# A state-space block with its FFN: one pass of TensorE per unit, the scores in three PSUM banks, y beside the states

## The reference, cut to what matters

```python
h = layernorm(x) * (1 + ca) + sa                      # x: (4, 512, 256)
proj = h @ W_in.T                                     # x, B, C, z, A_log
xBC = conv over 4 taps along l, per channel, + conv_b
a = -softplus(A_log)                                  # 32 heads
Lm = exp(segsum(a))                                   # l x s, lower triangle
M = einsum('blhn,bshn,bhls->bhls', Cm, Bm, Lm)        # 64 states per head
y = einsum('bhls,bshp->blhp', M, x) + D * x           # 8 channels per head
x = x + ga * ((y * silu(z + z_bias)) @ W_out.T)
h = layernorm(x) * (1 + cb) + sb
x = x + gb * (fwht(silu(h @ W1.T) * (h @ W3.T)) @ W2.T)
```

## Time and profile before

| what | value |
|---|---|
| median of 3 runs | 541.29 us (541.1 to 541.99) |
| the profiled execution's own time | 541.1 us |
| its span | 538.9 us |
| TensorE's granted clock, mean | 0.996 |
| busy: PE, DVE, ACT, POOL | 528.2, 455.3, 372.5, 241.0 us |

### The profile page before, as it was taken

One profiled execution on the slowest core, in us unless ns is written; L12 is line 12 of the kernel. 1 busy time (PEld: TensorE's weight loads), 2 busy tenths in 40 slices (PEclk: granted clock), 3 DMA queues, 4 the chain that ended last, 5 costly groups with the idle time before them and its releaser, 6 DMA issues.

```text
span 538.9 us, 19393 instructions
## 1 busy us (share of the span) xinstructions
PE 528.2 (98%) x7188; PEld 427.2 (79%) x7188; DVE 455.3 (84%) x746; ACT 372.5 (69%) x988; POOL 241.0 (45%) x465
## 2 busy tenths in 40 slices
PE   6999999999999999999999999999999999999997
PEld 3667777878878878877877877876889889889886
DVE  6999999999999999999999999999756657657342
ACT  1778998898898898898898898887534234234240
POOL 5863374776776775776775574484000000000000
PEclk9999999999999999999999999999999999999999
DMA  7737443432423425423423424566531322100101
GB/s 261 286 110 224 122 112 98 141 83 95 138 79 95 138 80 176 134 83 95 134 84 95 132 85 138 166 196 191 160 80 38 79 78 79 40 1 1 40 0 40
DMA packets 50289, 59.40 MB, mean 110 GB/s; under 512 B 8004, under 2 KB 44740, under 8 KB 49864
## 3 DMA queue, kind: packets, MB, share of 16 engines
q1 hardware_dynamic: 50248, 58.88, 36.0%
HBM read 48.75 MB, written 9.05 MB: 107 GB/s over the span
## 4 chain that ended last, share of the span: by engine, by line
PE 92%; DVE 4%; ACT 2%; issue 1%; DMA 1%; POOL 0%; SPq 0%; ACTq 0%; DVEq 0%; POOLq 0%
PE ps L371 20%; PE ps L372 20%; PE ps L373 20%; PE ps L550 10%; PE ps L531 6%; PE ps L600 4%; PE ps L586 3%; PE ps L569 3%; PE ps L667 3%; DVE acc L1177 2%; PE ps L396 1%; PE ps L613 1%; DMA u_sb<-in_u 1%; PE ps L426 1%; PE ps L677 1%
## 5 line engine op out<-in xcount | busy, mean ns | idle before, releaser
L1177 DVE SCALAR_TENSOR_TENSOR acc<-ps,cw_dve,acc 128x511 f32<-128x511 f32 (+2 forms) x384 | 257.8, 741 | 3.5 <-ACT acc L834 3.0
L868 ACT ACTIVATE decay<-sums,p_slot 128x128 f32<-128x128 f32 (+1 forms) x512 | 147.0, 370 | 2.2 <-ACT p_slot L943 1.0
L1478 POOL TENSOR_TENSOR sums<-sums,far_above 128x256 f32<-128x256 f32 x128 | 96.0, 753 | 117.4 <-DMA sums<-packed_sums 111.0
L834 ACT ACTIVATE acc<-ps,cw_act 128x512 f32<-128x512 f32 x128 | 93.0, 776 | 28.5 <-PE ps L600 26.4
L371 PE MATMUL ps<-ht_hi,wg_hi 128*128 128x512 f32 x256 | 107.1, 419 | 0.1
L372 PE MATMUL ps<-ht_lo,wg_hi 128*128 128x512 f32 x256 | 101.2, 395 | 0.0
L373 PE MATMUL ps<-ht_hi,wg_lo 128*128 128x512 f32 x256 | 101.2, 395 | 0.0
L1003 ACT ACTIVATE silu_sb<-ps 128x512 f32<-128x512 f32 x32 | 19.2, 599 | 77.8 <-PE ps L373 77.8
L1165 DVE TENSOR_TENSOR mix<-ps,decay 128x768 f32<-128x768 f32 x64 | 60.9, 952 | 6.1 <-PE ps L550 5.2
L1404 POOL TENSOR_TENSOR rstd<-vareps,minus_half 128x4 f32<-128x4 f32 x8 | 8.4, 1048 | 119.4 <-DVE vareps L1059 117.1
L550 PE MATMUL ps<-acc 64*64 64x128 f32 (+1 forms) x2048 | 57.6, 249 | 0.8
(11 more groups left out here) (143 smaller groups left out, 889.8 us busy)
## 6 DMA issues: line engine op xcount, KB each, us to landing
sums<-packed_sums SPq DMA_DIRECT2D x256, 96.0 KB, 2.7
wg_raw<-in_w_bc SPq DMA_DIRECT2D x8, 512.0 KB, 4.2
y_parts<-yt_sb SPq DMA_DIRECT2D x64, 64.0 KB, 2.0
stage<-y_parts SPq DMA_DIRECT2D x32, 128.0 KB, 2.8
u_sb<-in_u SPq DMA_DIRECT2D x4, 512.0 KB, 4.4
stage<-in_w SPq DMA_DIRECT2D x1, 2048.0 KB, 11.6
x_channels<-acc SPq DMA_DIRECT2D x8, 256.0 KB, 2.6
ee<-running_sums SPq DMA_DIRECT2D x8, 256.0 KB, 3.7
```

The lines of the kernel that those rows point to most:

```text
L834: af(acc[:, b % 2, t, :], ps[:, PROJ_BANK[t], :], ACT.Identity, bias=cw_act[:, t, 1:2], scale=cw_act[:, t, 0:1]).then_inc(s[f"tap_a{t}"], 1)
L868: i = af(decay[:, j, own], sums[:, j, own], ACT.Exp, scale=-1.0, bias=p_slot[:, b * CH + n, j:j + 1])
L1177: stt(a[:, d:], ps[:, PROJ_BANK[t], 0:L - d], cw_dve[:, t, TAPS - 1 - d:TAPS - d], a[:, d:], ALU.mult, ALU.add).then_inc(s[f"taps{t}"], 1)
L1478: gp.tensor_tensor(v, v, far, ALU.add).then_inc(s["masked"], 1)
```

## The change

PE goes through its three forms once per unit: the two transposes of q, projections 1, 0, 3, 2, states of q, inter and intra of r, and all scores of q in one block. The scores of both pairs go to banks 2, 3 and 7 (`place` gives each piece its columns; the same map is used for the decays and the mixed scores). Inside the block the two row halves of the array run the pieces in different orders, and a wait on the new semaphore `spare` keeps them from one bank. The first transposes go to bank 0, ahead of projection 0, which waits for their copy; y goes to bank 6, next to the second transposes and the states. DVE mixes a whole unit at once, 1024 and 512 columns, at the beginning of the next step but one. ACT and POOL have new orders. Some lines are left out below.

```diff
+SCORE_BANKS = [2, 3, 7]
+SPARE = [(0, 1), (1, 1), (2, 1), (3, 1), (2, 0), (3, 0)]
...
+        def place(j, k, h):
+
+            p, a = divmod(j, 2)
+            if p == 0:
+                return a * BANK + k * PW + NS * (1 - h)
+            if (k, h) == (0, 0):
+                return a * BANK + 2 * PW
+            return 2 * BANK + a * 2 * P + (P if h == 0 else NS * k)
...
+                if t == 0 and not (isinstance(n, int) and n == 0):
+                    pe.wait_ge(s["bt_ev"], 2 * n - 1)
...
-            def b_transposes(q, b, p, first):
+            def b_transposes(q, b, p):
+
                 pe.wait_ge(s[f"taps{p}"], 3 * q + 3)
-                if not first or p:
-                    pe.wait_ge(s["bt_ev"], 2 * q + p)
-                if not first and p == 0:
-                    pe.wait_ge(s["st_copy"], 2 * q)
+                if p:
+                    if not (isinstance(q, int) and q < 2):
+                        pe.wait_ge(s["yt_ev"], q - 1)
+                    if not (isinstance(q, int) and q == 0):
+                        pe.wait_ge(s["st_copy"], 2 * q)
                 for c in range(CH - 1):
-                    i = nc.tensor.transpose(ps[:, 6, c * P:(c + 1) * P],
+                    i = nc.tensor.transpose(ps[:, 6 if p else PROJ_BANK[0], c * P:(c + 1) * P],
                                             acc[:, b % 2, p, c * P:(c + 1) * P], ident)
                 i.then_inc(s["bt"], 1)
...
-            def scores(q, b, p, first):
-
-                pe.wait_ge(s[f"taps{p}"], 3 * q + 3)
-                pe.wait_ge(s[f"taps{2 + p}"], 3 * q + 3)
-                if not first or p:
-                    pe.wait_ge(s["mixed"], 2 * q + p)
+            def scores(q, b):
+
+                for t in range(GT):
+                    pe.wait_ge(s[f"taps{t}"], 3 * q + 3)
+                if isinstance(q, int) and q == 0:
+                    pe.wait_ge(s["xtok_ev"], 2 * B)
+                    pe.wait_ge(s["gate_ev"], 1)
                 else:
-                    pe.wait_ge(s["xtok_ev"], 2 * B)
+                    pe.wait_ge(s["mixed"], 2 * q)
                 pe.sem_inc(s["pe_waits"], 1)
...
+                spare = [(1, c, h) for c, h in SPARE]
+                rest = [(1, 0, 0), (1, 1, 0)] + [(0, c + e, h) for c in (0, 2) for h in range(2) for e in range(2)]
+                orders = (spare + rest, rest + spare)
+                for n in range(len(rest) + len(spare)):
+                    if n == len(rest):
+                        pe.wait_ge(s["spare"], 2 * q + 2)
+                        pe.sem_inc(s["pe_waits"], 1)
+                    for a in range(2):
+                        p, c, h = orders[a][n]
+                        own = slice(NS * a, NS * (a + 1))
+                        at = h if c % 2 == 0 else 1 - h
+                        bank, o = divmod(place(2 * p + a, c // 2, h), BANK)
+                        i = mm(ps[NS * at:NS * (at + 1), SCORE_BANKS[bank], o:o + P - NS * h],
+                               acc[own, b % 2, p, c * P + NS * h:c * P + NS * (h + 1)],
+                               acc[own, b % 2, 2 + p, c * P + NS * h:(c + 1) * P],
+                               start=True, stop=True)
+                        if n >= len(rest) + len(spare) - 2:
+                            i.then_inc(s["score"], 1)
+                        elif a == 0 and len(spare) - 2 <= n < len(spare):
+                            i.then_inc(s["spare"], 1)
...
-            def inter(q, b, first):
+            def inter(q, b):
 
                 pe.wait_ge(s["st_copy"], 2 * q + 2)
-                if first:
-                    pe.wait_ge(s["gate_ev"], 1)
+                if not (isinstance(q, int) and q == NG * B - 1):
+                    pe.wait_ge(s["bt_ev"], 2 * q + 4)
                 else:
                     pe.wait_ge(s["yt_ev"], q)
...
+                b_transposes(q, bq, 0)
+                b_transposes(q, bq, 1)
                 proj(g, b, 1)
-                states(r, br)
-                scores(r, br, 1, False)
-                b_transposes(q, bq, 0, False)
                 proj(g, b, 0)
                 proj(g, b, 3)
                 proj(g, b, 2)
-                inter(r, br, isinstance(r, int) and r == 0)
+                states(q, bq)
+                inter(r, br)
                 intra(r, br)
-                scores(q, bq, 0, False)
-                b_transposes(q, bq, 1, False)
...
             proj(0, 1, 1)
-            proj(0, 1, 0)
+            b_transposes(0, 0, 0)
             x_transposes(3, 0)
             x_transposes(3, 1)
+            b_transposes(0, 0, 1)
+            proj(0, 1, 0)
             proj(0, 1, 3)
-            b_transposes(0, 0, 0, True)
             proj(0, 1, 2)
-            scores(0, 0, 0, True)
-            b_transposes(0, 0, 1, True)
+            states(0, 0)
+            scores(0, 0)
...
+            b_transposes(last, B - 1, 0)
+            b_transposes(last, B - 1, 1)
             z_project(0, 0)
-            states(q, B - 2)
-            scores(q, B - 2, 1, False)
-            b_transposes(last, B - 1, 0, False)
-            inter(q, B - 2, False)
+            states(last, B - 1)
             pe.wait_ge(s["ld_wo"], 16)
             out_project(0, 0)
             pe.wait_ge(s["bfly"], 6)
             pe.wait_ge(s["ld_cst"], 16)
             w2_transform(0)
-            b_transposes(last, B - 1, 1, False)
             w2_transform(1)
-            scores(last, B - 1, 0, False)
+            inter(q, B - 2)
             intra(q, B - 2)
-            states(last, B - 1)
+            scores(last, B - 1)
             w2_transform(2)
-            scores(last, B - 1, 1, False)
-            inter(last, B - 1, False)
             w2_transform(3)
             norm2_transposes(0, 0)
+            inter(last, B - 1)
             intra(last, B - 1)
...
-                    act.wait_ge(s["mixed"], 2 * q + j // 2 - 1)
+                    act.wait_ge(s["mixed"], 2 * q)
...
                 act.wait_ge(s["state"], 4 * r + 4)
+                if not (isinstance(r, int) and r == 0):
+                    act.wait_ge(s["intra"], JH * r)
...
+                if not (isinstance(r, int) and r == NG * B - 1):
+                    act.wait_ge(s["state"], 4 * r + 8)
                 if not (isinstance(before, int) and before == 0):
                     act.wait_ge(s[f"st_y{half}"], 32 * before)
-                nc.scalar.copy(yt_sb[:, half, :], ps[:, 7, 0:2 * P]).then_inc(s["yt_ev"], 1)
+                nc.scalar.copy(yt_sb[:, half, :], ps[:, 6, 0:2 * P]).then_inc(s["yt_ev"], 1)
...
-                state_copies(r)
-                if b == 1:
-                    head_rows(g)
-                decays(q, bq, 0, False)
-                decays(q, bq, 1, False)
+                b_evacuate(q, 0)
+                b_evacuate(q, 1)
+                decays(r, (b - 2) % B, 3, isinstance(r, int) and r == 0)
                 if b == 0:
                     act.wait_ge(s["cwa"], g + 1)
                 last_tap(g, b, 1)
                 last_tap(g, b, 0)
                 if b == 0:
                     coefficients(g, 2)
+                if b == 1:
+                    head_rows(g)
                 if split:
                     act.wait_ge(s["ld_wg"], (g + 2) * 16)
                     nc.scalar.copy(wg_hi[:, 1], wg_raw[:, 1]).then_inc(s["w_high_act"], 1)
                     nc.scalar.copy(wg_hi[:, 0], wg_raw[:, 0]).then_inc(s["w_high_act"], 1)
+                decays(q, bq, 0, False)
+                decays(q, bq, 1, False)
                 decays(q, bq, 2, False)
-                b_evacuate(q, 0)
                 last_tap(g, b, 3)
                 last_tap(g, b, 2)
                 y_evacuate(r, b % 2, gr * 2 + (b - 2) % B // 2)
+                state_copies(q)
                 if b == B - 1 and not last:
                     coefficients(g + 1, 0)
-                b_evacuate(q, 1)
-                if not last:
-                    decays(q, bq, 3, False)
...
             last_tap(0, 1, 1)
             x_evacuate(2, 1)
-            last_tap(0, 1, 0)
             act.wait_ge(s["xn_done"], CH * B)
             af(e_rows, sums_t[:], ACT.Exp, scale=-1.0).then_inc(s["e_rows"], 1)
-            decays(0, 0, 1, True)
-            x_evacuate(3, 0)
             act.wait_ge(s["wz_split"], 2)
             act.wait_ge(s["st_sums"], 64)
             act.wait_ge(s["st_zero"], 1)
             b_evacuate(0, 0)
+            x_evacuate(3, 0)
             x_evacuate(3, 1)
+            b_evacuate(0, 1)
+            decays(0, 0, 1, True)
+            last_tap(0, 1, 0)
+            decays(0, 0, 2, True)
             last_tap(0, 1, 3)
             last_tap(0, 1, 2)
-            decays(0, 0, 2, True)
-            b_evacuate(0, 1)
-            decays(0, 0, 3, True)
+            state_copies(0)
...
+            b_evacuate(last, 0)
+            b_evacuate(last, 1)
+            decays(r, B - 2, 3, False)
             silu_gate(0)
-            state_copies(r)
-            b_evacuate(last, 0)
-            decays(r, B - 2, 3, False)
```

(83 more changed lines are left out.)

23 lines of the change are left out of this document (5 added, 18 removed).

## The result

The kernel after takes 548.94 us (median of 4 runs, 548.54 to 550.68), the kernel before 541.64 us beside it. The ratio is 1.0137, 95% interval 1.0107 to 1.0167: 7.4 us slower. The span went from 538.9 to 546.9 us. The forecast was 548.0 us, between 538 and 553.

A forecast was written before the change was run, and what follows sets the result against it. PE was taken to bound the kernel, with DVE nearly as full; new waits would close loops through PE, ACT and DVE. Start 2.4, units 1.0 and end 3.5 gave +6.9 on 541.1: 548.0 us, range 538 to 553.

The forecast's parts named there:

- PE's saving, 0.5 us a unit: PE, each unit: merged scores and projections mean fewer array-form changes; own work falls by about 0.5 to 9.55 us.
- The loop through PE and ACT, 10.03: Each unit: second transposes, four projections, states, inter, intra, two last taps, y and state copies close a 10.03 us loop.
- The loop through DVE and ACT, 10.06: Each unit: undivided mix, twelve exponentials, two last taps and DVE's taps close a 10.06 us loop.
- The unit with the weights' copies, 10.2 once per group: Unit where ACT copies the next group's weights: 10.2 us, once in four; with it 29 units cost 1.0 us more.
- put at nothing, POOL: POOL's four weight splits run ahead of the unit's masks; masks are wanted a unit later, so no cost.
- Start +2.4: Kernel's start: ACT's last tap 0 of unit 1 moves later, delaying unit 2's last tap 3 by 2.4 us, bounds 0 and 3.
- End +3.5: From last unit's last tap 3 to first FFN matmul: 27.5 us against 24.0, +3.5, bounds +1 and +5.
- S: Time mark at the kernel's end: the last unit's last tap 3 on ACT, 358.11 us in the kernel before.
- the sum of +6.9: Whole kernel: start 2.4, units 1.0 and end 3.5 added to the profiled 541.1 us, giving 548.0.
- The rival "PE's saving is realised": Units: waits land in cover, DVE's work sets the period, 11.6 us less, ends +5.9, about 535.4; chance of faster 0.17.

The follow-up runs named there:

- dummy matmuls: Kernel after plus sixteen matmuls, their result unused, in PE's idle stretch ahead of the last unit's states: 548.67 us, ratio 1.0127.
- The kernel with both loops opened and the tap 2 moved: Kernel after with two decay buffers, and ACT's y copy and state copies between last tap 3 and last tap 2: 541.75 us, ratio 0.9999.
- the kernel with the new end: Kernel after with Silu ahead of unit 30's last decays and the last states behind the first out_project: 546.56 us, ratio 1.0085.
- the one with all edits: Kernel after with two decay buffers, copies ahead of last taps 3 and 2, last tap 0 of unit 1 earlier, Silu earlier, last states later: 545.28 us.
- the best pair with the end: Kernel after with two decay buffers, copies between last taps 3 and 2, Silu earlier, last states behind first out_project: 541.55 us, ratio 0.9995.

## Why the prediction was right

**PE's saving, 0.5 us a unit: none of it reached the time.** Scores in one block took 1.56 where I had 1.5, and there was no loss from the unequal pairs. PE's own work, forecast 9.55, is at most 9.60 by its timeline: the work went away and came back as 0.44 us of standing, forecast 0.4 to 0.5.

**The loop through PE and ACT, 10.03: shown.** With the other loop gone the period was still 10.07, and ACT's wait stood at intra (0.56).

**The loop through DVE and ACT, 10.06: shown, to about 0.1.** With the first one open, two copies more in it made 10.63. What I overlooked is a third loop close under these two, through PE, ACT and DVE, which shows only when both are open (9.97); it didn't touch the forecast.

**The unit with the weights' copies, 10.2 once per group: mis-sized.** The 29 units cost +0.3 instead of +1.0. Units with the copies on ACT measured 10.04 and 10.05, like their neighbours. What did cost something, 0.6 us once, was put at nothing, POOL: in the unit of 10.63 PE waited for POOL's weight splits, and these stood behind the mask of head 3 in the queue, which came at 118.23 there and at 113.96 before. Head 3's row is loaded later now, since its exponentials are; that this is the reason wasn't tested.

**Start +2.4: +2.3**; tap 0 ended at 56.18 (forecast 56.1), tap 3 began at 68.55 (forecast 68.6).

**End +3.5: mis-sized, +5.4.** The gates ended at 369.19 = S + 8.4 (8.5), sixteen exponentials at 376.66 = S + 15.9 (14.8). I had left out the table load of 1.28 us between Silu and the exponentials, +1.1, and what PE's idle 4.18 us does to the clock: out_project +2.0, of which 1.3 lay on the path to the statistics (with the dummy matmuls the statistics came 1.5 earlier). From the statistics to the FFN it took 390.19 - 380.05 = 10.1 where I had 10.8, -0.7; with +0.2 of small waits that makes the 1.9. Moving Silu and the states gave 2.4 us of the 5.4 back.

The errors of the units (-0.7) and of the end (+1.9) have opposite signs, and the sum of +6.9 stood against 8.0 in the span. That it came out within a microsecond or so is in part luck: the mechanism in the units was right, but in the end over a microsecond came from a fall of the clock that I hadn't reckoned with, and it doesn't come in every such kernel. **The rival "PE's saving is realised"** was refuted by its own condition: it needed both loops under 9.8. But it is nearer than its chance said. The kernel with both loops opened and the tap 2 moved runs its units in 9.84 us, and is as fast as the kernel before. It gains 29 x 0.23 = 6.7 us in the units and pays 2.2 at the start and 4.2 at the end. No version beat the kernel before by more than a measurement tells. DVE's own work is 9.7 us a unit in that kernel (98.22 us busy in 99.74, at 9.84 a unit) and stands in the way of more.

## What to carry to other kernels

When an edit takes waits between blocks off the bounding engine by putting more behind one semaphore, write each closed loop over the in-order queues (who waits for whom until the same instruction comes again) and add its turns. The longest loop is the period, whatever each engine's busy share says. Opening one of several equal loops shows nothing; open them in pairs. And where an edit leaves an idle stretch of some microseconds on TensorE, give the forecast a second figure, with the matmuls behind it at the lower clock (here 5.66 us for 3.69).

## What wasn't expected of the hardware

PE's clock fell behind idle stretches of 2.35, 2.52, 3.09 and 4.18 us (granted 0.66, 0.88, 0.83, 0.69 in the windows around), and stayed at 1.00 around stretches of 2.39 and 3.11 us in the kernel with the new end and of 3.03 us in the one with all edits. The length of the idle stretch alone doesn't tell which it will be. Filling or shortening one such stretch moved the fall to the next in two kernels (dummy matmuls, and the best pair with the end); in the other three with the new end there was no fall in that part at all.
